# A decoder layer whose attention loops are rolled over one pair of head groups, changed to two pairs per turn with the last four pairs written out

## The chip, the cores and the metric

The kernel runs on one core of a Trainium2 chip. The metric is the device time of one execution in microseconds (us). The core has five engines that run their own instruction streams and meet only at semaphores: TensorE (PE in the profile; its weight loads are PEld), VectorE (DVE), ScalarE (ACT), GpSimd (POOL) and SyncE (SP, which only issues DMAs here).

## The reference

The layer has three stages. Each is followed by a residual and a layer norm.

1. A phase-memory mixer on `x` [8, 512, 256], with cumulative sums over the tokens.
2. Cross-attention, 16 heads of 16 channels, queries from `x`, keys and values from a context [8, 1601, 256]. Its softmax runs over the queries, so each key row is normalized by itself:

```python
sm = einsum('nlhd,nshd->nlhs', q, k) / sqrt(D)
sm = softmax(sm, axis=1)          # over the 512 queries l
attn = einsum('nlhs,nshd->nlhd', sm, v)
```

3. A feed-forward with 8 experts, the two best of each token.

## The kernel before

Each stage is a block of its own. The change touches only the second one, the attention block. The 16 heads are cut into groups of four (`GH = 4`), which gives `NG = 32` groups over the 8 batches. The unit of all loops is a **pair of groups**, so there are `NG // 2 = 16` pairs. The 1601 context rows of a group are 13 tiles of 128 rows (`ST = 13`, the last has 65 rows), so a pair has `N_TILE = 26` tiles. The work on one tile is:

- PE, `scores` (L1039): four matmuls, one for each head, keys on the partitions and 512 queries along the row. Two heads go to one of three score buffers in PSUM (`score_buf`, `SCORE_BUFS = 3`). The wait on `exp_done` makes PE stay within these three.
- DVE (L1102): the negated maximum over the queries, two heads in one instruction.
- ACT (L1194): `exp` of each head with its sum beside it. The profile shows each as an ACTIVATE and an ACTIVATION_READ_ACCUMULATOR.
- DVE `inverse` (L1071): the reciprocal of the sums. POOL (L1166): the value tile times these, `v_scaled`.
- PE `pv` (L1007): values times probabilities, three tiles behind the scores (`LAG = 3`). At the end of a group DVE copies the sum to `attn` (L1116) and SP stores it.

For the first `FILLED = 13` pairs the engines do something else besides (`fill`): between the score matmuls PE makes the keys and values of a later unit of context (L1022, L1027), DVE reads them (L1082, L1090), and POOL splits the keys in three parts and stores them (L1133 to L1150). The last three pairs have none of this.

Every engine has its own loop over the same pairs. PE and DVE share `rounds`: three tiles of the first pair ahead of the loop, a loop over the pairs 0 to 12 with fill, a loop over the pairs 13 and 14 without, and the last pair written out. A turn of `rounds` begins at tile 3 of a pair and ends with tile 2 of the next. POOL has two loops (0 to 12 and 13 to 15) and ACT one loop over all 16, both beginning at tile 0. SP's loop already goes over two pairs in a turn and isn't changed. A wait on a count that depends on the loop's variable takes a register instruction ahead of it, which computes the count; a wait on a constant doesn't. At the end of a turn an engine runs a register step, a compare-and-branch back to the first instruction of the body, and one or two register steps more. There is no barrier between the engines at the end of a turn.

Of the kernel before, what the change touches and what calls it, by code (L numbers as in the profile page):

```python
# [51 lines left out]
def decoder_layer(nc, a, out):  # L52
# [12 lines left out]
    NG = B * G  # L65
# [35 lines left out]
    with ExitStack() as top:  # L101
# [3 lines left out]
        def tensors(ctx):  # L105
            def sb(name, shape, dt=F32):
                return ctx.enter_context(nc.sbuf_tensor(name, shape, dt))
            return sb
# [35 lines left out]
        def wait_alone(eng, *waits):  # L144


            waits = [(s, n) for s, n in waits if not isinstance(n, int) or n > 0]
            for _, n in waits:
                if not isinstance(n, int):
                    eng.to_reg(n)  # L150
            eng.wait_ge(consts_made, 1)
            for s, n in waits:
                eng.wait_ge(s, n)
# [26 lines left out]
        with ExitStack() as ctx:  # L180
# [237 lines left out]
            with nc.Block() as block:  # L418
                @block.sync
                def _(sp):  # L420
                    for tile, src in consts:
                        sp.dma_start(tile, src).then_inc(consts_loaded, 16)

                    def load(b, h):
                        for c in range(C):
                            sp.dma_start(xt[:, h, c, 1:L + 1], a["xT"][b, c]).then_inc(xt_loaded[h], 16)
                        sp.dma_start(xin[:, h], a["x"][b].rearrange("(t p) d -> p t d", p=P)).then_inc(xt_loaded[h], 16)

                    for h in range(2):
                        load(h, h)  # L430
                    with sp.Fori(1, B // 2) as it:
                        for h in range(2):
                            b = 2 * it + h

                            sp.wait_ge(kv_ready, b - 1)
                            sp.wait_ge(x2bo_ready, b - 1)
                            load(b, h)
                    first_units_sp(sp)
# [413 lines left out]
        with ExitStack() as ctx:  # L852
# [3 lines left out]
            N_SUB, N_TILE = 2 * SUBS, 2 * ST  # L856
            LAG = 3
# [14 lines left out]
            FILLED = UNITS - FIRST_UNITS  # L872
# [25 lines left out]
            def free(k, buffer_of, it):  # L898


                rounds, k = divmod(k, len(buffer_of))
                round_, p = last_user(k, buffer_of)
                return len(buffer_of) * it + len(buffer_of) * (rounds + round_) + p + 1 + CREDIT

            def head_free(k, i, it):
# [3 lines left out]
                round_, p = last_user(k, score_buf)  # L909
                return 2 * N_SUB * it + 2 * (N_SUB * (rounds + round_) + p) + i + 1 + 2 * CREDIT  # L910

            def rounds(eng, tile_step):


                for tile in range(LAG):
                    tile_step(tile, 0, False)
                for first, end, fill in ((0, FILLED, True), (FILLED, NG // 2 - 1, False)):
                    with eng.Fori(first, end) as it:
                        for tile in range(LAG, N_TILE + LAG):
                            tile_step(tile, it, fill)  # L920
                for tile in range(LAG, N_TILE + LAG):
                    tile_step(tile, NG // 2 - 1, False)

            def is_over(tile, it):

# [2 lines left out]
            with nc.Block() as block:  # L928
# [65 lines left out]
                def rows_of(t):  # L994
                    return P if t < ST - 1 else TAIL
# [126 lines left out]
                @block.gpsimd  # L1122
                def _(pool):
                    def unit_step(p, at, it):

                        u = it + FIRST_UNITS
                        kb = p % 2
                        before = STEPS_OF_PAIR * (4 * it + p)
                        co, s0 = p // 2, (p % 2) * KC
                        if at == 0:  # L1130

                            wait_alone(pool, (k1_stored[kb], 16 * (2 * it + p // 2)), (items_read, ITEMS * it + 2 * p + 2))
                            pool.tensor_scalar(k1_out[:, kb, 0], k1_f[:], 1.0, None, ALU.mult).then_inc(unit_steps, 1)  # L1133
                        elif at == 1:
                            pool.wait_ge(unit_steps, before + 2)
                            pool.tensor_tensor(k1_rest[:], k1_f[:], k1_out[:, kb, 0], ALU.subtract) \
                                .then_inc(unit_steps, 1)
                        elif at == 2:
                            wait_alone(pool, (unit_steps, before + 3))
                            pool.tensor_scalar(k1_out[:, kb, 1], k1_rest[:], 1.0, None, ALU.mult).then_inc(unit_steps, 1)  # L1140
                        elif at == 3:
                            pool.wait_ge(unit_steps, before + 4)
                            pool.tensor_tensor(k1_out[:, kb, 2], k1_rest[:], k1_out[:, kb, 1], ALU.subtract) \
                                .then_inc(unit_steps, 1)
                            wait_alone(pool, (unit_steps, before + 5))
                            pool.dma_start(k_parts[:, u, co * P:(co + 1) * P, s0:s0 + KC].rearrange("n p s -> p n s"),
                                           k1_out[:, kb]).then_inc(k1_stored[kb], 16)
                        elif p == 3:
                            wait_alone(pool, (items_read, ITEMS * (it + 1) + 1))
                            pool.dma_start(v_all[u].rearrange("g p f -> p g f"),  # L1150
                                           v1_out[:].rearrange("p g t f -> p g (t f)")).then_inc(v1_stored, 16)


                    STEPS_OF_PAIR = 4
                    pool.wait_ge(pads_zeroed, 1)
                    pool.sem_inc(unit_steps, 1)
                    pool.sem_inc(items_read, 1)
                    for first, end, fill in ((0, FILLED, True), (FILLED, NG // 2, False)):
                        with pool.Fori(first, end) as it:
                            for tile in range(N_TILE):  # L1160
                                h, t = divmod(tile, ST)
                                r, pb = rows_of(t), prob_buf[tile]

                                pool.wait_ge(pv_done, free(tile, prob_buf, it))
                                pool.wait_ge(inv_ready, N_TILE * it + tile + 1)
                                pool.tensor_tensor(  # L1166
                                    v_scaled[0:r, pb, :, 0:DH], vst[0:r, h, t, :].rearrange("p (j d) -> p j d", j=GH),
                                    inv[0:r, pb].rearrange("p (j o) -> p j o", o=1).to_broadcast([r, GH, DH]), ALU.mult) \
                                    .then_inc(v_scaled_ready, 1)
                                if fill:  # L1170
                                    for p in range(4):
                                        if 2 <= tile - FILL_AT[p] < 7:
                                            unit_step(p, tile - FILL_AT[p] - 2, it)
                    for i in range(2):
                        pool.wait_ge(k1_stored[i], 32 * FILLED)
                    pool.wait_ge(v1_stored, 16 * FILLED)

                @block.scalar
                def _(act):
                    act.wait_ge(pads_zeroed, 1)  # L1180
                    act.sem_inc(exp_done, 2 * CREDIT)
                    with act.Fori(0, NG // 2) as it:
                        for tile in range(N_TILE):
                            h, t = divmod(tile, ST)
                            r, pb = rows_of(t), prob_buf[tile]

                            act.wait_ge(pv_done, free(tile, prob_buf, it))
                            for sub in range(2):
                                k = 2 * tile + sub
                                sbuf = score_buf[k]  # L1190
                                act.wait_ge(max_ready, N_SUB * it + k + 1)
                                for i in range(2):
                                    j = 2 * sub + i
                                    act.activation(probs[0:r, pb, j, :], psum[0:r, 2 * sbuf + i, :], ACT.Exp,  # L1194
                                                   bias=neg_max[0:r, sbuf, i:i + 1], scale=-1.0,
                                                   accum_out=sums[0:r, pb, j:j + 1]).then_inc(exp_done, 1)

        sb = tensors(top)
        w2_all = sb("w2_all", [P, E, HC, D])
# [654 lines left out]
```

## Time and profile before

| | |
|---|---|
| median of 3 runs | 2395.06 us (2393.85 to 2396.78) |
| the profiled execution, its own time | 2394.24 us |
| its span, first to last instruction | 2392.5 us |
| attention, from ACT's first `exp` to the end of its last | 511.4 to 1666.8 us, 1155.4 us |
| one pair of groups in it | 70.4 to 73.5 us |

A row of a group of instructions reads: line, engine, operation, output from inputs, shapes, count, then busy time, mean ns of one, and the idle time of the engine just before them with what ended it. A q behind an engine's name (PEldq, ACTq) means its sequencer, which takes instructions in order and runs a little ahead of the engine itself; register and branch instructions run there and count as busy for no engine.

### The profile page before, as it was taken

What the parts mean: (1) busy time and instruction counts of PE and PEld (TensorE: products, weight loads), DVE (VectorE), ACT (ScalarE), POOL (GpSimd) and SP (SyncE); (2) the same over time, 40 slices, a digit from 0 to 9 for tenths busy, and PEclk for the clock granted to TensorE, in tenths of its full rate; (3) what the DMA queues carried; (4) which work ended last, traced back from release to release, by engine and by line L of the source; (5) the groups of instructions that cost most, each with busy time, mean ns of one, the idle gap of its engine ahead of it and who ended that gap; (6) DMA issues with size and microseconds to landing.
All of it is one profiled execution on the core that took longest, in us unless ns stands there. A gap on an engine that the chain in (4) does not pass through costs nothing. (4 is left out here: it accounts for less than half of the span.)

```text
span 2392.5 us, 40765 instructions
## 1 busy us (share of the span) xinstructions
PE 2009.6 (84%) x10318; PEld 1030.3 (43%) x10318; DVE 1842.9 (77%) x2913; ACT 1557.2 (65%) x4288; POOL 845.4 (35%) x985
## 2 busy tenths in 40 slices
PE   5888675739999999999999998887662999999994
PEld 2334332412322222322222321111552999999993
DVE  5999996429999999999999999897562555555554
ACT  4555443429999999999999999998220333333334
POOL 1034444614444444444444442110474322332231
PEclk9989887869999999999999999999765999999997
DMA  3011110474666756656756665641852222222224
GB/s 105 18 49 39 53 64 31 150 121 83 108 123 115 142 109 114 114 106 132 127 105 126 103 127 85 97 61 31 278 186 90 39 37 35 35 38 36 35 36 153
DMA packets 131723, 217.38 MB, mean 91 GB/s; under 512 B 20418, under 2 KB 102978, under 8 KB 131554
## 3 DMA queue, kind: packets, MB, share of 16 engines
q1 hardware_dynamic: 104514, 146.55, 33.2%
q0 software_dynamic: 27168, 70.35, 10.4%
q8 instruction: 17, 0.28, 0.1%
q14 instruction: 24, 0.20, 0.0%
HBM read 138.10 MB, written 78.72 MB: 91 GB/s over the span
## 5 line engine op out<-in xcount | busy, mean ns | idle before, releaser
L1194 ACT ACTIVATE probs<-psum,neg_max 128x512 f32<-128x512 f32 (+1 forms) x1664 | 1110.8, 772 | 71.8 <-DVE neg_max L1102 70.3
L1102 DVE TENSOR_REDUCE neg_max<-psum 128x2 f32<-128x1024 f32 (+1 forms) x832 | 986.0, 1214 | 97.1 <-PE psum L1039 88.9
L1039 PE MATMUL psum<-qst,kst 96*128 96x512 bf16 (+1 forms) x1664 | 543.9, 395 | 110.7 <-ACT probs L1194 72.9
L1194 ACT ACTIVATION_READ_ACCUMULATOR probs<-psum,neg_max 128x1 f32 (+1 forms) x1664 | 488.1, 293 | 0.0
L1007 PE MATMUL psum<-probs,v_scaled 128*32 128x512 f32 (+1 forms) x3328 | 455.1, 620 | 0.0
L1039 PEld LDWEIGHTS psum<-qst,kst 96*128 96x128 bf16 (+1 forms) x1664 | 130.5, 98 | 717.6 <-ACT probs L1194 657.3
L1689 ACT ACTIVATE hid<-psum,b 128x128 f32<-128x128 f32 x568 | 162.0, 368 | 393.4 <-PE psum L1662 393.4
L1166 POOL TENSOR_TENSOR v_scaled<-vst,inv 128x64 f32<-128x64 f32 (+1 forms) x416 | 120.9, 291 | 704.5 <-DVE inv L1071 698.4
L1723 POOL DMA_INDIRECT sums_all<-y_out,dest x71 | 154.4, 2175 | 381.0 <-DVE y_out L1768 375.2
L1662 PE MATMUL psum<-xst,w 128*128 128x128 f32 x2272 | 266.9, 276 | 0.0
L1662 PEld LDWEIGHTS psum<-xst,w 128*128 128x128 f32 x2272 | 261.1, 193 | 0.1
L1672 PE MATMUL psum<-w,hid 128*128 128x256 f32 x1136 | 256.9, 379 | 0.0
L1672 PEld LDWEIGHTS psum<-w,hid 128*128 128x128 f32 x1136 | 210.4, 190 | 25.7
L1768 DVE SCALAR_TENSOR_TENSOR y_out<-psum,weight,b_scaled 128x256 f32<-128x256 f32 x71 | 34.3, 484 | 184.5 <-issue 178.0
L1007 PEld LDWEIGHTS psum<-probs,v_scaled 128*32 128x32 f32 (+1 forms) x3328 | 66.6, 109 | 122.3 <-issue 105.4
L1027 PE MATMUL psum<-ct,xwk 128*128 128x448 f32 x208 | 96.3, 544 | 9.7 <-DMA ct<-in_ctxT 9.7
L1738 DVE COPY w<-w_all 128x2048 f32 x71 | 97.4, 1372 | 0.0
L1022 PE MATMUL psum<-xwv,ct 128*128 128x256 f32 x364 | 93.6, 379 | 0.0
L1739 DVE COPY w<-w_all 128x2048 f32 x71 | 86.2, 1214 | 0.0
L495 PE MATMUL psum<-xt,wpv 128*128 128x512 f32 x64 | 42.6, 829 | 44.5 <-DVE y L720 44.5
L1737 DVE COPY b<-b_cols 128x8 f32 x71 | 30.3, 426 | 60.8 <-DVE xst L1750 59.8
L1022 PEld LDWEIGHTS psum<-xwv,ct 128*128 128x128 f32 x364 | 69.1, 190 | 17.9
(227 smaller groups left out, 2337.6 us busy)
## 6 DMA issues: line engine op xcount, KB each, us to landing
kst<-k_parts SPq DMA_DIRECT2D x384, 112.0 KB, 6.1
k_parts<-k_out POOLq DMA_DIRECT2D x64, 336.0 KB, 2.9
w_all<-in_W SPq DMA_DIRECT2D x16, 1024.0 KB, 10.9
ct<-in_ctxT SPq DMA_DIRECT2D x16, 896.0 KB, 4.7
v_all<-v_out POOLq DMA_DIRECT2D x16, 896.0 KB, 4.3
vst<-v_all SPq DMA_DIRECT2D x64, 224.0 KB, 8.5
qst<-q_parts SPq DMA_DIRECT2D x192, 64.0 KB, 5.5
rows_in<-xs SPq DMA_DIRECT2D x71, 129.0 KB, 2.0
```

The costliest lines, as they stand in the source:

```text
L1007: last = pe.matmul(psum[j * PAD:(j + 1) * PAD, 6, :], v_scaled[0:r, pb, j, :], probs[0:r, pb, j, :], start=t == 0, stop=t == ST - 1)
L1022: last = pe.matmul(psum[:, 7, (t % 2) * D:(t % 2 + 1) * D], ct1[:, k, t * P:(t + 1) * P], xwv[:, k, :], start=k == 0, stop=k == C - 1)
L1027: last = pe.matmul(psum[:, 7, 0:KC], xwk[:, part, co * P:(co + 1) * P], ct1[:, part, s0:s0 + KC], start=part == 0, stop=part == 1)
L1039: last = pe.matmul(psum[0:r, 2 * sbuf + i, :], kst[:, h, j, t * P:t * P + r], qst[:, h, j, :], start=True, stop=True)
L1102: v.tensor_reduce(neg_max[0:r, sbuf], psum[0:r, 2 * sbuf:2 * sbuf + 2], AX_X, ALU.min) \
L1166: pool.tensor_tensor(v_scaled[0:r, pb, :, 0:DH], vst[0:r, h, t, :].rearrange("p (j d) -> p j d", j=GH), inv[0:r, pb].rearrange("p (j o) -> ...
L1194: act.activation(probs[0:r, pb, j, :], psum[0:r, 2 * sbuf + i, :], ACT.Exp, bias=neg_max[0:r, sbuf, i:i + 1], scale=-1.0, accum_out=sums[0 ...
L1662: last = pe.matmul(psum[:, 2 + 2 * h + c // 4, (c % 4) * P:(c % 4 + 1) * P], w1[:, h, k, c * P:(c + 1) * P], xst[:, h, k, :], start=k == 0 ...
L1672: last = pe.matmul(psum[:, 6 + h, 0:D], hid[:, h, c, :], w2[:, h, c, :], start=c == 0, stop=c == HC - 1)
L1689: act.activation(hid[:, h, c], psum[:, 2 + 2 * h + c // 4, (c % 4) * P:(c % 4 + 1) * P], ACT.Relu, bias=b1[:, h, c:c + 1]).then_inc(h_read ...
L1723: pool.indirect_dma_start(sums_all, bass.IndirectOffsetOnAxis(dest[:, d, :], 0), y_out[:, h], None, compute_op=ALU.add).then_inc(y_added[h ...
L1738: v.tensor_copy(w1[:, half], w1_all[:, at].rearrange("p o c h -> p (o c) h")).then_inc(w1_ready, 1)
```

## The change

The loop over pairs becomes a helper, `in_pairs`, that PE, DVE, POOL and ACT all use. It runs 6 turns of two pairs each (0 to 11, all with fill), and then pair 12 with fill and pairs 13, 14 and 15 without are written out with constants in place of the loop's variable. The operations on data, their order on each engine, their shapes and the semaphore counts stay as they are.

```diff
+            def in_pairs(eng, group_pair):
+                with eng.Fori(0, FILLED // 2) as two:
+                    for i in range(2):
+                        group_pair(2 * two + i, True)
+                group_pair(FILLED - 1, True)
+                for it in range(FILLED, NG // 2):
+                    group_pair(it, False)
...
                 for tile in range(LAG):
                     tile_step(tile, 0, False)
-                for first, end, fill in ((0, FILLED, True), (FILLED, NG // 2 - 1, False)):
-                    with eng.Fori(first, end) as it:
-                        for tile in range(LAG, N_TILE + LAG):
-                            tile_step(tile, it, fill)
-                for tile in range(LAG, N_TILE + LAG):
-                    tile_step(tile, NG // 2 - 1, False)
+                def group_pair(it, fill):
+                    for tile in range(LAG, N_TILE + LAG):
+                        tile_step(tile, it, fill)
+
+                in_pairs(eng, group_pair)
...
-                    for first, end, fill in ((0, FILLED, True), (FILLED, NG // 2, False)):
-                        with pool.Fori(first, end) as it:
+                    def group_pair(it, fill):
...
+                    in_pairs(pool, group_pair)
...
-                    with act.Fori(0, NG // 2) as it:
+                    def group_pair(it, fill):
...
+                    in_pairs(act, group_pair)
```

## Rows read from the trace of the kernel before

**Rows 1.** The page: the span.

```profile
span 2392.5 us, 40765 instructions
```

**Rows 2.** Windows: all of attention, then two pairs, from first `exp` to first `exp`.

```profile
core 0: us, PE busy (x) PEld busy (x) DVE busy (x) ACT busy (x) POOL busy (x), PEclk, DMA share, GB/s
511.40:1666.80 1155.40, 1063.98 (x5547) 305.01 (x5550) 1075.95 (x1420) 1117.51 (x3328) 413.81 (x688) 0.97 0.60 106
950.84:1024.37 73.53, 70.14 (x365) 20.96 (x364) 68.12 (x92) 70.02 (x209) 30.72 (x48) 0.95 0.65 122
1024.37:1094.80 70.43, 65.62 (x352) 20.31 (x348) 68.00 (x91) 69.79 (x208) 29.50 (x47) 1.00 0.64 113
```

**Rows 3.** Waits, 600 to 1667 us: us in total, times, longest.

```profile
ACT probs L1194 <- DVE neg_max L1102: 24.2, 32, 1.4
```

**Rows 4.** ACT's loop control: whole trace, then the branch near 1093 us.

```profile
L1182 ACTq COMPARE_BRANCH  x16: 40/45/45, 592.2 to 1665.5; - x16
...
L1182 ACTq COMPARE_BRANCH  x1: 45/45/45, 1093.3 to 1093.3; - x1
```

**Rows 5.** ACT in order of time around that branch, and at tile 3.

```profile
1093.27 0.68 ACT L1194 ACTIVATE probs<-psum,neg_max 65x512 f32<-65x512 f32 x1 [0.51 <-DVE neg_max L1102]
...
1093.94 0.67 ACT L1194 ACTIVATE probs<-psum,neg_max 65x512 f32<-65x512 f32 x1
...
1094.80 0.69 ACT L1194 ACTIVATE probs<-psum,neg_max 128x512 f32<-128x512 f32 x1
...
1103.29 0.72 ACT L1194 ACTIVATE probs<-psum,neg_max 128x512 f32<-128x512 f32 x1
```

**Rows 6.** Loop control of PE and DVE within 1094.8 to 1166.72 us.

```profile
L918 PEldq COMPARE_BRANCH  x1: 208/208/208, 1099.7 to 1099.7; - x1
L918 PEldq FUSED_REGOPS  x1: 50/50/50, 1099.9 to 1099.9; - x1
L918 DVEq COMPARE_BRANCH  x1: 56/56/56, 1101.1 to 1101.1; - x1
```

**Rows 7.** PE and DVE in order of time behind their branches.

```profile
1100.80 0.60 PE L1039 MATMUL psum<-qst,kst 96*128 96x512 bf16 x2
...
1101.98 2.34 DVE L1102 TENSOR_REDUCE neg_max<-psum 128x2 f32<-128x1024 f32 x2
```

**Rows 8.** Lines, one pair (1094.8 to 1166.7 us): how many instructions a body has.

```profile
L1194 ACT ACTIVATION_READ_ACCUMULATOR probs<-psum,neg_max 128x1 f32 (+1 forms) x104 | 28.1, 270 | 0.0
...
L1007 PEld LDWEIGHTS psum<-probs,v_scaled 128*32 128x32 f32 (+1 forms) x216 | 4.3, 109 | 8.0 <-issue 7.1 <-POOL v_scaled L1166 1.0
```

**Rows 9.** Register steps of two waits of ACT and PE, the same pair.

```profile
L1191 ACTq ALU_OP  x51: 35/35/35, 1094.8 to 1161.9; - x51
...
L1038 PEldq ALU_OP  x106: 32/32/36, 1094.9 to 1166.0; - x106
```

**Rows 10.** DMA queues by kind: 505 to 700, then all queues of 700 to 1455 us.

```profile
q14 instruction: 6, 0.05, 0.1%
q8 instruction: 3, 0.05, 0.1%
...
q1 hardware_dynamic: 43056, 64.00, 55.3%
q0 software_dynamic: 5980, 23.75, 8.5%
```

**Rows 11.** The page: queues that carry instructions, and two transfers, issue to landing.

```profile
q8 instruction: 17, 0.28, 0.1%
q14 instruction: 24, 0.20, 0.0%
...
kst<-k_parts SPq DMA_DIRECT2D x384, 112.0 KB, 6.1
...
attn_all<-attn SPq DMA_DIRECT2D x128, 32.0 KB, 1.6
```

More of the change, by code:

```diff
@@ L910, in head_free @@
                 return 2 * N_SUB * it + 2 * (N_SUB * (rounds + round_) + p) + i + 1 + 2 * CREDIT
+            def in_pairs(eng, group_pair):
[5 more added lines that the diff above has]
+                    group_pair(it, False)
+            assert FILLED % 2 == 1
             def rounds(eng, tile_step):
```

## The prediction

> **What bounds the kernel now.** I read the windows first. Attention takes 1155.4 us of the span of 2392.5 us, and nothing else is touched, so the rest (1237.1 us of the span, and 1.7 us between the span and the execution's own time of 2394.24 us) stays [rows 1, 2]. In attention ACT is busy for 1117.5 us, TensorE for 1064 and VectorE for 1076 [rows 2]. ACT sets the pace, and the other two are so close behind that an interruption of either soon reaches it. A pair takes 70.43 us where the granted clock stays at 1.00 and 73.53 us where it is 0.95, with the same ACT work (69.8 and 70.0 us) [rows 2]. From the first branch of ACT to its last, 15 pairs later, it is 1073.3 us, so the mean pair is 71.55 us [rows 4].
>
> Then I asked what ACT waits for. Between 600 and 1667 us it is the row maxima of VectorE alone, 24.2 us in 32 waits [rows 3], two for each of 15 pairs. Both stand at the end of a pair: in the stretch shown ACT waits 0.51 us in the middle of the last tile, and loses about 0.2 us more before the next pair's first `exp`, which starts 0.86 us behind the last one where the usual distance is 0.66 [rows 5]. The code says why: `score_buf` gives the last half tile of a pair buffer 1, which was used two steps before and not three, so the ring of three is one short there. The change keeps this order. The reader is to see that the idle time at a pair's end is a data wait and not the price of a branch.
>
> **What the change removes.** PE and DVE run 15 turns now and 6 afterwards, ACT 16 and POOL 16 against 6. On PE a turn's end costs a branch of 0.208 us and a register step of 0.05, with small gaps from 1099.7 to about 1100.1 us [rows 6]. PE's next score matmuls start at 1100.80, behind the `pv` matmuls that were queued before the branch, so this is covered [rows 7]. DVE's branch (0.056 us, at 1101.1) lies under work queued ahead of it; its next reduction starts at 1101.98 [rows 6, 7]. ACT's branch, 0.045 us at 1093.3, is issued while the `exp` of 1093.27 has only begun [rows 4, 5]. If a cover were gone, PE would be worth 0.4 us for each of 9 turns removed, 3.6 us, and that is the upper bound of this gain. I take 0. The register steps for waits are 0.035 us each on ACT and 0.032 on PE [rows 9]; four of the 16 pairs lose them, and they run beside matmuls and `exp`s. Again 0. The second pair of a turn needs its count from `2 * two + 1`, which is a different constant in the same step, so nothing is added.
>
> **What the change adds: longer bodies.** This is where I expect the time to move. ACT's body is 104 `exp` and 104 accumulator reads [rows 8] and a register step for each of its 78 waits, of which the one line shows 51 [rows 9], so 208 + 78 + 3 for the loop = 289 instructions. Two pairs make 578. PE's has 208 score instructions (104 matmuls with their loads), 416 for `pv`, 88 for the fill, and some 145 register steps, of which L1038 has 106 [rows 9] (that window shows 216 loads for `pv`, a few from the neighbours [rows 8]): about 857, doubled 1714. DVE's, counted in the code (52 reductions, 26 reciprocals, 13 others, some 96 steps), is 187, doubled 374. POOL's is some 145, doubled 290.
>
> Instructions come by DMA, and the trace shows when. In 505 to 700 us, the first pass through the bodies, queue q14 moved 6 packets and q8 3; in 700 to 1455 us, ten more pairs, neither queue appears at all [rows 10]. So each body of today is held inside its engine and replayed. The packets are 0.20 MB / 24 = 8.3 KB on q14 and 0.28 / 17 = 16.5 KB on q8 [rows 11]. On q8 three packets for PE's 857 instructions make about 280 in a packet, so one of q14 holds about 140. The whole program is fetched once, packet after packet as the engines come to it, which is the manner of a small store. What the store of an engine holds no row says; what it surely holds is 3 packets for ACT (289 instructions, cut by the packets' edges) and about 5 for PE. Twice that is 5 or more packets on ACT, 4 on DVE and POOL, and 7 or 8 on PE, and one ahead of each. I judge it likelier than not that ACT's is over, and that DVE's and PE's are at the edge or over, because no body of today comes near those sizes. If a body doesn't fit, its first packet is gone when the branch goes back, and the engine stands until it is read again. The packets after it are fetched while the one before runs (a packet of 140 lasts ACT some 34 us), as in the first pass, so a turn pays once per engine. There are 6 turns and so 5 branches back. The code written out behind the loop is streamed without a stall.
>
> [...]
>
> **The price of a miss.** The trace before has none, so it is bounded by the nearest rows: from issue to landing a small store takes 1.6 us, and a key load in the busy queues of attention 6.1 us [rows 11]. The queues of DMA are 55% busy here [rows 10]. One packet is small, so it is nearer to the first: I take 3.5 us, and keep 1.6 and 6.1.
>
> ACT: its branch is at 1093.3 and the next `exp` starts at 1094.80, so 1.5 us are covered [rows 4, 5]. Lost: 3.5 - 1.5 = 2.0 us (0.1 to 4.6).
>
> DVE: its branch is at 1101.1, with the next reduction at 1101.98 [rows 6, 7]. With a miss this starts at 1104.6, 2.6 us late. It has two scores' maxima; the first ends 1.17 us after its start, at 1103.15, and ACT uses it at 1103.29 [rows 5, 7]: 0.15 us of slack. Lost: 2.5 us (0.6 to 5.0). A miss of PE falls in the same stretch: its branch at 1099.7 plus 3.5 is 1103.2 against 1100.80 today, 2.4 us late, so the scores come before DVE is back. Without DVE's miss it would cost 2.2 us itself. Together I take 2.5.
>
> POOL: `v_scaled` is read by `pv` three tiles later, behind scores that wait for the `exp` of the tile after next; at 2.7 us a tile (70.43 / 26 [rows 2]) that is some 4 us, which covers 3.5. Queued behind it are only the splits and two DMAs. 0, and 2 at 6.1.
>
> The clock: every stand of more than about 2 us idles PE too, and the pair with clock 0.95 took 3.1 us more than the pair at 1.00 [rows 2]. I take half of it, 1.5 us a turn (0 to 3).
>
> Sum for a turn: 2.0 + 2.5 + 1.5 = 6.0 us, times 5 = 30 us. On 2394.24 us this gives 2424 us, and the runs' median is 0.8 us above the profiled execution, so 2425 us. Lower end: (0.1 + 0.6) x 5 = 3.5, 2399. Upper end: (4.6 + 5.0 + 2 + 3) x 5 = 73, 2468; for the likely case alone 2405 to 2450.
>
> **The rivals.** What a measurement can tell from no change is 0.2%, 4.8 us, so 2390.3 to 2399.9 us counts as the same.
>
> *Only ACT is over.* Its body is the one that grows past twice anything a q14 engine holds today, while DVE's 374 is 1.3 times ACT's present 289. Then 5 x (2.0 + 1.0 for the clock) = 15 us: 2410 us. For it: the sizes. Against it: the packet ahead takes room too. [...]
>
> *Everything fits, the change does nothing.* For it: no body of today is ever refetched, so the limit is not in sight [rows 10]. The covered branches give 0: 2395 us, between 2391 and 2398.
>
> *Faster, by the clock.* If everything fits and the removed branches shift PE's idle moments so that dips in the clock are missed, pairs go towards the 70.43 us of the undisturbed one from their mean of 71.55 [rows 2, 4]: 1.1 us for 15 pairs, 17 us, 2378 us, at most. A third of it, 6 us, 2389 us, is what I could believe. It decides when more than four of the pairs lose their dip. Against it: the idle at the pair's end, which brings the dip, comes from the buffer ring and stays.
>
> **How the numbers follow.** ACT with DVE or PE over the edge: 0.5 (2425). Only ACT: 0.22 (2410). Nothing: 0.2 (2395). Faster: 0.08 (2389). The predicted time is that of the first. Of the first two some 0.02 may stay under 2399.9, if a fetch takes only 1.6 us. So slower 0.7, same 0.22, faster 0.08. A range that reaches from the foot of "nothing" to the top of the likely case, 2392 to 2450, leaves out about 0.07 below and 0.07 above.
>
> **What the changed profile would show.** q14 packets in every turn between 700 and 1400 us, five or so for ACT alone, and q8 packets too if PE is over. Five gaps of about 2 us on ACT at the start of every other pair, ended by the issue and not by VectorE's maxima, and five of some 2.5 us near tile 3 that end with a late maximum. The pairs inside a turn stay at 70.4 to 72 us, the written-out pairs as well. Wrong it would be if the instruction queues stay silent, if a miss costs under 1.5 us, or if the gaps fall on other places than the branches back.

## The result: 2409 us, slower, because VectorE reads its loop again at every branch back

The changed kernel took 2409.34 us (median of 4 runs, 2406.01 to 2411.13) against 2395.15 us (4 runs of before, 2393.85 to 2396.78). The ratio is 1.0057, 95% interval 1.004 to 1.0075, so 10 to 18 us were lost. The forecast was 2425 us: the direction was right, and the size was more than twice too large. 2409 us is what the rival gave in which only one engine's body is too long (2410), but it named the wrong engine (ACT), so that this nearness is luck.

First the windows of the changed kernel: the whole of attention, a pair behind a branch back in which the granted clock stayed at 1.00, then the pair before another branch back and the pair behind it.

```profile
span 2406.8 us, 39692 instructions
```

```profile
512.40:1681.90 1169.50, 1071.43 (x5543) 305.30 (x5546) 1077.07 (x1420) 1119.18 (x3328) 413.89 (x688) 0.96 0.59 105
812.84:885.19 72.35, 66.21 (x356) 20.32 (x348) 67.56 (x91) 69.90 (x208) 29.69 (x47) 1.00 0.66 125
1031.94:1103.67 71.73, 67.81 (x364) 20.65 (x356) 68.12 (x92) 69.79 (x208) 29.48 (x47) 0.98 0.62 111
1103.67:1178.04 74.37, 69.14 (x360) 20.70 (x356) 68.16 (x92) 70.22 (x209) 30.40 (x48) 0.95 0.64 122
```

Attention takes 1169.5 us against 1155.4 [rows 2], which is 14.1 of the 14.3 us that the span grew. The counts of operations and the busy times of ACT, VectorE and GpSimd are those of before. The pair behind a branch back takes 74.37 us, and the pair ahead of it 71.73, near the mean of before, 71.55 us [rows 4]. It is so in every turn: four of the five pairs behind a branch back take 74.4 to 75.0 us, with a granted clock of 0.93 to 0.95, and the fifth 72.35 us with a clock of 1.00; the second pair of each of these turns takes 71.1 to 72.1 us.

The queues of DMA by kind, 700 to 1380 us, in which the kernel before has no instruction packets [rows 10]:

```profile
q1 hardware_dynamic: 38167, 56.42, 54.0%
q0 software_dynamic: 5280, 20.99, 8.3%
q14 instruction: 70, 0.57, 0.3%
```

The forecast's first sign is there, 70 packets of 8 KB on q14. There is none on q8: TensorE's doubled body is not fetched again.

Now loop control of all four engines in 1100 to 1114 us of the changed kernel. A row reads: engine's sequencer, operation, count, duration in ns, and the start of its first and last. The pair of COMPARE_BRANCH and the FUSED_REGOPS that follows it is what to read: this register step is the first instruction at the branch's target.

```profile
L915 ACTq COMPARE_BRANCH  x1: 45/45/45, 1100.9 to 1100.9; - x1
L915 ACTq FUSED_REGOPS  x1: 59/59/59, 1103.4 to 1103.4; - x1
...
L915 POOLq COMPARE_BRANCH  x1: 50/50/50, 1105.8 to 1105.8; - x1
...
L915 PEldq COMPARE_BRANCH  x1: 215/215/215, 1108.0 to 1108.0; - x1
L915 PEldq FUSED_REGOPS  x1: 59/59/59, 1108.4 to 1108.4; - x1
L915 POOLq FUSED_REGOPS  x1: 59/59/59, 1108.4 to 1108.4; - x1
...
L915 DVEq COMPARE_BRANCH  x1: 63/63/63, 1109.4 to 1109.4; - x1
L915 DVEq FUSED_REGOPS  x1: 74/74/74, 1112.3 to 1112.3; - x1
```

And the same step of VectorE in the kernel before, behind its branch at 1101.1 [rows 6]:

```profile
L918 DVEq FUSED_REGOPS  x1: 63/63/63, 1101.4 to 1101.4; - x1
```

From branch to target it is 2.5 us on ACT, 2.6 on GpSimd and 2.9 on VectorE, against 0.3 us on VectorE before. On TensorE the branch takes 0.215 us, against 0.208 before [rows 6]. So three of the four bodies are read again, and what each stand is worth depends on what covers it. VectorE and ACT in order of time (a bracket is idle time before the instruction and what ended it):

```profile
1109.50 0.66 DVE L1127 COPY attn<-psum 128x512 f32<-128x512 f32 x1
1112.43 2.36 DVE L1113 TENSOR_REDUCE neg_max<-psum 128x2 f32<-128x1024 f32 x2 [2.27 <-issue]
```

```profile
1101.52 0.67 ACT L1205 ACTIVATE probs<-psum,neg_max 65x512 f32<-65x512 f32 x1
...
1103.67 0.69 ACT L1205 ACTIVATE probs<-psum,neg_max 128x512 f32<-128x512 f32 x1 [1.39 <-DVE neg_max L1113]
...
1113.69 0.69 ACT L1205 ACTIVATE probs<-psum,neg_max 128x512 f32<-128x512 f32 x1 [1.89 <-DVE neg_max L1113]
```

VectorE stands idle for 2.27 us for want of instructions, and the `exp` that needs its maximum comes 1.89 us late. ACT itself had its first instruction back at 1103.4 us, just before the `exp` at 1103.67, and that `exp` is put down to a maximum of VectorE: a wait of 1.4 us that pairs of the kernel before have too. ACT's waits in 600 to 1682 us, to be set beside the 24.2 us in 32 waits of before [rows 3]:

```profile
ACT probs L1205 <- DVE neg_max L1113: 35.4, 43, 2.0
```

That is 11.2 us more, of the 14.1. Most of it is the wait of 1.89 us shown above, at tile 3: it stands there in each of the five pairs behind a branch back, 1.8 to 2.0 us long, 9.3 us together, and in no pair of the kernel before.

Of what the prediction said that the changed profile would show, the packets came, and the five gaps near tile 3 as well. Five gaps of about 2 us on ACT that end with the issue did not: at one of the five branches back the wait is put down to the issue, 1.21 us, and at the other four to VectorE's maxima.

### The profile page after: what moved, and what is told of

It is laid out like the page before. It is cut to its first block and busy times, and to the rows that moved or that the text cites. A ratio compares the mean times of both kernels' runs of the same rounds, so it can differ in the third digit from the quotient of the medians.

```text
span 2406.8 us, 39692 instructions
## 1 busy us (share of the span) xinstructions
PE 2017.0 (84%) x10318; PEld 1030.4 (43%) x10318; DVE 1845.0 (77%) x2913; ACT 1559.0 (65%) x4288; POOL 845.3 (35%) x985
## 5 line engine op out<-in xcount | busy, mean ns | idle before, releaser
L1205 ACT ACTIVATION_READ_ACCUMULATOR probs<-psum,neg_max 128x1 f32 (+1 forms) x1664 | 477.7, 287 | 0.0
```

## The experiments

All are timed against the kernel before in the same session. Where one says that an engine has "the loops of before", its turns are those of the old code. Theory A, formed from the rows above: all of the loss comes from VectorE's refetch, and ACT's and GpSimd's are covered. The rivals are mostly the forecast's own terms.

**One engine at a time.** `in_pairs` on one engine (ACT in e1, VectorE in e2, GpSimd in e3, TensorE in e4) and the old loops on the other three, by this helper, and by one loop over all 16 pairs on ACT:

```diff
+            def one_by_one(eng, group_pair):
+                last = NG // 2 - (group_pair.__qualname__.find('rounds') >= 0)
+                for first, end, fill in ((0, FILLED, True), (FILLED, last, False)):
+                    with eng.Fori(first, end) as it:
+                        group_pair(it, fill)
+                for it in range(last, NG // 2):
+                    group_pair(it, False)
```

> Only ACT runs two pairs per turn with the last four written out; PE, DVE and POOL keep the loops of before. Theory A (the lost time is DVE's refetch at its branch back, ACT's refetch is nearly covered by the wait at a pair's end): 0 to 5 us over before, 2395 to 2400, with ACT standing some 2.4 us at 5 branches. Rival B (the forecast's own term: ACT's refetch costs 2.0 us and the clock 1.0 us a turn): 2410.

Measured: 2396.66 us, ratio 0.9997 (0.9988 to 1.0006). No loss that can be measured. ACT does refetch, in every turn (packets in 700 to 1380 us, and its loop control in 600 to 1370 us):

```profile
q14 instruction: 27, 0.22, 0.2%
```

```profile
L915 ACTq COMPARE_BRANCH  x5: 45/45/45, 664.0 to 1237.0; - x5
L915 ACTq FUSED_REGOPS  x5: 59/59/64, 666.4 to 1239.5; - x5
```

Its stand is 2.4 to 2.5 us at every branch, and no cost of it shows. At two of the five branches back it is the stand that ACT waits for longest:

```profile
666.59 0.69 ACT L1223 ACTIVATE probs<-psum,neg_max 128x512 f32<-128x512 f32 x1 [1.23 <-issue]
```

That is no more than pairs of the kernel before wait there for a maximum of VectorE, up to 1.4 us [rows 3].

> Only DVE runs two pairs per turn with the last four written out. Theory A: 5 times some 2.6 us, all of the loss, 2406 to 2410. Rival B (DVE's refetch is half of it or less): 2400 or less. Rival C (the loss needs several engines standing at once): 2395.

Measured: 2407.09 us, ratio 1.0037 (1.0023 to 1.0051), 5 to 12 us. It carries most of the loss, alone. Theory A had all of the loss. VectorE's packets in 700 to 1380 us, and its loop control in 600 to 1370 us, where branch and target are 3.0 us apart:

```profile
q14 instruction: 22, 0.18, 0.1%
```

```profile
L915 DVEq COMPARE_BRANCH  x5: 63/63/63, 672.4 to 1253.1; - x5
L915 DVEq FUSED_REGOPS  x5: 74/74/80, 675.4 to 1256.2; - x5
```

> Only POOL runs two pairs per turn with the last four written out. All theories: POOL stands some 2.6 us at 5 branches, the time is that of before, 2393 to 2397. If v_scaled is in truth late for pv: up to 5 us more.

Measured: 2397.62 us, ratio 1.0002 (0.9993 to 1.0011), with 21 packets on q14. The median lies 0.6 us above the range expected, and by the ratio it is that of before. GpSimd stands at its branches all the same, 2.5 to 3.0 us. The packets of the three add up: 27 + 22 + 21 = 70, those of the changed kernel.

> Only PE runs two pairs per turn with the last four written out. Theory A: PE's doubled body stays resident, no instruction packets on q8 after its first turn, 2393 to 2397. Rival (PE's own loop costs time even when resident, or the written-out pairs do): over 2398. Rival (fewer branches help PE): under 2392.

Measured: 2396.62 us, ratio 0.9998 (0.9989 to 1.0007), no instruction packets in the same window. The forecast that saved branches are worth nothing because they were covered holds for TensorE.

**The same changed kernel with VectorE left out (e8).**

> PE, ACT and POOL as in the changed kernel, DVE with the loops of before. Theory A: ACT and POOL stand at their 5 branches, PE doesn't, 2395 to 2401. Rival (the engines' stands add up, 13.6 against the 9 of DVE alone): 2399 to 2403.

Measured: 2395.17 us, ratio 0.9997 (0.9988 to 1.0007). TensorE, GpSimd and ACT together lose nothing that can be measured. Theory A stands from both sides, VectorE alone and all but VectorE.

**Is it the length of the body, or where it lies?** In the trace of e2 VectorE's packets of 8 KB come when it is about 84, 217 and 340 instructions into its body of 372. By these places, and this is an estimate, a packet holds some 128 instructions, the body begins 45 behind an edge, and it touches 4 packets. Two more packets come at each branch back, the first 1.0 to 1.3 us behind the branch, the second 3.6 to 3.7 us behind it, when VectorE is 8 instructions into the body: the next packet is fetched ahead here, while the engine is still in the one before. So it is five in each turn, the 4 that are touched and the one ahead. In e3 GpSimd's packets come some 151 and 279 instructions into its body of 288, which by the same estimate begins some 105 behind an edge and touches 4 as well. ACT's body in the kernel before has 288 instructions too; by the places of its packets in e1, the last two some 348 and 477 instructions behind the branch, it begins some 35 behind an edge and touches 3, and it was held [rows 10]. 88 instructions more ahead of VectorE's loop should put its start just behind an edge, and then it touches 3 and the one ahead is the fourth (e7):

```diff
                     v.memset(v_scaled[:], 0.0).then_inc(pads_zeroed, 1)
+                    for _ in range(88):
+                        v.sem_inc(spare, 1)
                     v.sem_inc(attn_copied, 1)
```

> As the run with only DVE over two pairs, with 88 increments of an unused semaphore put ahead of DVE's first tile, which move its loop body to the edge of an instruction packet, so that its 372 instructions touch 3 packets and not 4. Theory A (DVE's store holds 4 packets, one of them the packet fetched ahead): no refetch after the first turn, the branch back takes 0.3 us, 2393 to 2400. Rival (the length of 372 itself is too much, wherever it lies): the refetches stay, 2404 to 2410.

Measured: 2395.68 us, ratio 1.0 (0.9991 to 1.0009). The loss is gone with 88 instructions more in the program. No instruction packets are left in 700 to 1380 us, and the step behind the branch is back at 0.3 us (loop control in 600 to 1370 us):

```profile
L916 DVEq COMPARE_BRANCH  x5: 56/56/74, 673.4 to 1245.9; - x5
L916 DVEq FUSED_REGOPS  x5: 74/74/80, 673.7 to 1246.2; - x5
```

The same shift in the whole changed kernel (e10):

> The changed kernel with the 88 increments ahead of DVE's first tile. Theory A: the time of all but DVE, 2393 to 2399, with ACT and POOL still refetching. Rival (the four engines' longer bodies cost together, whatever DVE does): 2400 or more.

Measured: 2395.08 us, ratio 0.9998 (0.9989 to 1.0007), with 48 packets on q14, which is ACT's 27 and GpSimd's 21. This is the changed kernel without its loss, and it is no faster than the kernel before.

**TensorE moved over its own edge (e9).** In e4's first turn q8's packets of 16 KB come some 216, 472 and 731 instructions behind TensorE's branch at 484.1 us. By these places, an estimate again, a packet holds some 256 instructions, and the body of 1711 should touch 7 packets and end a few tens of instructions short of the next. 64 increments of the unused semaphore ahead of its first tile, in the changed kernel:

> The changed kernel with 64 increments of an unused semaphore ahead of PE's first tile, which move its body of 1711 instructions so that it touches 8 packets of 16 KB and not 7. Theory (PE holds 8 packets, one of them the one fetched ahead): q8 packets in every turn, PE stands some 3 us at each of 5 branches, in the same stretch as DVE; 0 to 8 us over the changed kernel, 2410 to 2418. Rival (PE's store is larger): no q8 packets, 2408 to 2411.

Measured: 2414.28 us, ratio 1.0077 (1.0064 to 1.009), 4.9 us above the changed kernel by the medians of two sessions; the intervals of the two ratios overlap, so that a cost of the second stand is likely and not shown. The refetch itself is plain in the trace (packets in 700 to 1380 us, TensorE's loop control in 600 to 1390 us):

```profile
q8 instruction: 41, 0.67, 0.5%
q14 instruction: 70, 0.57, 0.4%
```

```profile
L916 PEldq COMPARE_BRANCH  x5: 3343/3662/4186, 671.5 to 1259.3; - x5
L916 PEldq FUSED_REGOPS  x5: 59/59/68, 675.7 to 1263.0; - x5
```

From one branch back to the next (818.8 to 965.5 us) it is 9 packets on q8, which fits 8 that are touched and one ahead. On TensorE the refetch shows inside the branch itself, 3.3 to 4.2 us in place of 0.2. In this trace TensorE is back at 675.7 us and VectorE at 675.9, and in the fifth turn at 1263.0 and 1263.6: the two stands lie over each other, which fits that the second adds little.

**Does anything add to VectorE's loss (e11 with ACT, e12 with GpSimd)?** The changed kernel lost 0.57% and VectorE alone 0.37%.

> DVE and ACT over two pairs per turn, PE and POOL as before. The changed kernel is 13.6 us slower and DVE alone 9. If ACT's refetch adds the rest (it spoils the short waits at a pair's end, and the clock with them): 2408 to 2411. If not: 2403 to 2407.

> DVE and POOL over two pairs per turn, PE and ACT as before. If POOL's refetch adds the rest (v_scaled later, pv later behind DVE's stand): 2408 to 2411. If not: 2403 to 2407.

Measured: 2407.51 us, ratio 1.0049 (1.0036 to 1.0062), and 2408.24 us, ratio 1.0046 (1.0031 to 1.006). Both ratios lie between 1.0037 and 1.0057, and all four intervals overlap. Which engine adds the last few us, if one does, stays open.

**No loop at all, and then a regular ring.** The first run (e5) writes all 16 pairs out on the four engines:

```diff
+            def written_out(eng, group_pair):
+                for it in range(NG // 2):
+                    group_pair(it, it < FILLED)
```

> All 16 pairs written out on PE, DVE, ACT and POOL, no loop. Theory A (only branches back that miss cost; new code is fetched ahead in time): 2391 to 2397. Rival (long straight code costs by its fetches, or register steps were worth something): over 2400, or under 2390.

Measured: 2396.04 us, ratio 1.0003 (0.9994 to 1.0012), with 26 packets on q8 and 31 on q14 in 700 to 1380 us. Straight code that is fetched all the time costs nothing here that can be measured, and neither do 15 branches back of the kernel before, whose bodies were held [rows 10].

With the pair's number known everywhere, the score buffers need not begin anew at each pair. The second run (e6) counts the half tiles through. The first two lines below choose PE's buffer, with the same edit on VectorE and ACT; the others are the count that PE waits for:

```diff
-                        r, sbuf = rows_of(t), score_buf[k % N_SUB]
+                        r, sbuf = rows_of(t), (N_SUB * it + k) % SCORE_BUFS
...
-                round_, p = last_user(k, score_buf)
-                return 2 * N_SUB * it + 2 * (N_SUB * (rounds + round_) + p) + i + 1 + 2 * CREDIT
+                return 2 * N_SUB * it + 2 * (N_SUB * rounds + k - SCORE_BUFS) + i + 1 + 2 * CREDIT
```

> As all pairs written out, and the score buffers go round 0, 1, 2 over the whole of attention, without the step of two at each pair's end. Theory (the idle time at a pair's end comes from that step and brings the clock's dips): ACT's 0.74 and 0.2 to 1.5 us at each of 15 pair ends go, 2365 to 2380. Rival (PE and DVE are so close behind ACT that the slack is used elsewhere): 2385 to 2395.

Measured: 2365.19 us (4 runs, 2363.38 to 2367.15), ratio 0.9871 (0.9856 to 0.9886), 27 to 34 us faster than before. Since e5, which lacks only the ring, takes the time of before, this gain is the ring's. Its windows, all of attention and two pairs:

```profile
514.60:1640.30 1125.70, 1049.27 (x5551) 303.33 (x5550) 1077.46 (x1420) 1113.81 (x3328) 414.90 (x688) 0.99 0.61 109
944.44:1014.17 69.73, 66.64 (x360) 20.54 (x356) 68.18 (x92) 69.68 (x211) 30.17 (x47) 1.00 0.68 130
1014.17:1083.91 69.74, 66.66 (x360) 20.53 (x356) 68.17 (x92) 69.69 (x211) 30.20 (x47) 1.00 0.65 115
```

ACT at the end of a pair, where the kernel before waits twice [rows 5]:

```profile
1012.84 0.79 ACT L1222 ACTIVATE probs<-psum,neg_max 65x512 f32<-65x512 f32 x1
...
1013.51 0.80 ACT L1222 ACTIVATE probs<-psum,neg_max 65x512 f32<-65x512 f32 x1
...
1014.17 0.80 ACT L1222 ACTIVATE probs<-psum,neg_max 128x512 f32<-128x512 f32 x1
```

From 600 to 1640 us ACT has no wait on VectorE left. The pairs 1 to 12 take 69.7 us each, with ACT busy throughout, and the granted clock in the two shown is 1.00, over all of attention 0.99 against 0.97 before [rows 2]. Of 71.55 us a pair [rows 4], 1.8 us went, and 30 us over attention.

## Why the prediction was right and where it was wrong

- **The saved branches are worth nothing: right.** The ratios of e4, e5, e8 and e10 are all within 0.1% of before.
- **Bodies too long are read again at each branch back: right,** and with 5 branches back. What each engine holds could not be read in the trace before; the shifts of e7 and e9 show where refetching begins for these bodies. By the packets in 700 to 1380 us and the places given above, VectorE's 372 instructions were held where they touch 3 packets (e7, none on q14) and read again where they touch 4 (e2, 22); GpSimd's 288 were read again in 4 (e3, 21), and ACT's 288 held in 3 [rows 10]; TensorE's 1711 were held in 7 (e4, none on q8) and read again in 8 (e9, 41). So the body counts here by the packets that it touches and not by its length. With the one ahead this makes 4 packets of some 128 instructions that stay on VectorE, and 8 of some 256 on TensorE, an estimate from these counts and places.
- **TensorE over the edge: wrong in the changed kernel,** right by 64 instructions in e9. It moved no time in the sum, since it had been put in the same stretch as VectorE's stand.
- **The price of a fetch, 3.5 us: a little high.** It is 2.4 to 3.0 us on ACT, GpSimd and VectorE, and 3.3 to 4.2 us on TensorE.
- **VectorE's term, 2.5 us a turn: a little high.** Where the granted clock stays at 1.00, a pair behind a branch back takes 72.35 us in the changed kernel, against 70.43 before [rows 2]: 1.9 us, for one pair. e2 loses 9 us by its ratio, 1.8 us a turn, with 1.1 to 2.4 in its interval, the clock's part included.
- **ACT's term, 2.0 us a turn: this is the step that failed.** Measured: nothing clear of noise (e1, between 2.9 us faster and 1.4 us slower over all five turns). The sum took the shortest cover, the 1.5 us between branch and next `exp` at one pair end [rows 4, 5], and a price of 3.5. In the rows ahead of the prediction there was one pair end of many, and I read its 1.5 us as the rule. There the next pair's first `exp` starts 0.86 us behind the last one, and only 4 of the 15 pair ends of the trace before are that short; the distance goes up to 2.16 us, and its mean is 1.58:

```profile
1022.21 0.67 ACT L1194 ACTIVATE probs<-psum,neg_max 65x512 f32<-65x512 f32 x1
...
1024.37 0.69 ACT L1194 ACTIVATE probs<-psum,neg_max 128x512 f32<-128x512 f32 x1 [1.40 <-DVE neg_max L1102]
```

In e1 the distance at the five branches back is 2.00 to 2.15 us. So a stand of 2.5 us ends inside the wait for VectorE's maximum, or little behind the usual end of it.

- **The clock's term, 1.5 us a turn: too high, the second part of the miss.** It was added as if it came in full on top of both stands. That every stand of more than about 2 us idles TensorE is not what the runs showed. ACT's stands of 2.4 to 2.5 us in e1 left no gap of TensorE over 0.6 us in the 3.5 us behind the branch, and the granted clock of the pair behind each is 0.98 to 1.00; behind GpSimd's stands of 2.5 to 3.0 us in e3 it is 0.98. Behind VectorE's in the changed kernel it is 0.93 to 0.95 four times and 1.00 once. All that the changed kernel lost, stands and clock together, is 13.7 us, 2.7 a turn (1.9 to 3.6). Less the 1.9 us of VectorE's stand this leaves some 0.8 us, an estimate, for the clock and whatever else adds.
- **GpSimd covered: right** (e3).
- So 2.0 + 2.5 + 1.5 should have been 0 + 1.9 + about 0.8, and the range held the result because of the rivals in it, which was luck as far as the sum goes.
- **A reading that was not exact.** The 32 waits of ACT [rows 3] are not two for each of 15 pairs: 15 stand in the middle of the last tile, 11 at the next pair's first `exp`, and 6 at its third or fifth. That they come from the step in the buffer ring was right: with the regular ring of e6 none is left.

## What to carry to other kernels

Before a loop is unrolled, count each engine's instructions per turn and look in the trace for instruction packets in the steady part: where there were none here [rows 10], all bodies were held, and the branches cost nothing that could be measured (e5, without any, ratio 1.0003). A longer body cost time that could be measured here only on VectorE (e2, ratio 1.0037), whose branch back no wait covered, and whether it was read again could hang on where it began in its packets (22 packets in e2, none in e7). If the turn's end shows idle time, ask first for the data wait that stands there: here it was one step of a buffer ring, worth 30 us, where the branches were worth none.

## What was not expected of the hardware

- 88 instructions without any use, put ahead of a loop, made one kernel 9 us faster by the ratios (e2 to e7) and another 14 us (the changed kernel to e10), and 64 on another engine brought refetches of 3.3 to 4.2 us (e9).
- Code that runs straight through cost nothing measurable: in e5 the four engines took 57 packets in 680 us and the time was that of before (ratio 1.0003).
- On TensorE a refetch lengthens the COMPARE_BRANCH itself (3.3 to 4.2 us in e9), on the other three the branch stays at 45 to 64 ns and the gap stands behind it.
- Two bodies of 288 instructions fared differently: ACT's of before, in 3 packets, was held [rows 10], and GpSimd's of e3, in 4, was fetched again at every turn (21 packets on q14 in 700 to 1380 us).
